# Layer 0's attention stream: every block of probabilities turned by a transpose, and the output projection over two groups of heads instead of four

## The chip, the core and the metric

The kernel runs on one NeuronCore of a Trainium2 chip. The core's engines work side by side and wait for each other by semaphores: TensorE (PE, matmuls into PSUM; PEld is its weight load), VectorE (DVE), ScalarE (ACT), GpSimd (POOL) and SyncE (SP, which issues DMAs). The metric is the device time of one execution in microseconds, the median of several runs. TensorE's clock is granted at one of two levels, 2.4 GHz (shown as 1.00) or 1.2 GHz (shown as 0.50).

## What is computed

A decoder of two layers on 4 sequences of 256 tokens, width 256, all in float32. Layer 0, which the change touches, begins with causal self-attention of 16 heads of width 16 and cross-attention of 8 heads of width 32:

```python
# self-attention, dk = 16, after rotary embedding of Q and K
scores = jnp.einsum('bhqd,bhkd->bhqk', Q, K) / dk ** 0.5
scores = jnp.where(causal, scores, -jnp.inf)
probs = jax.nn.softmax(scores, axis=-1)
attn = jnp.einsum('bhqk,bhkd->bhqd', probs, V)
attn = attn.swapaxes(1, 2).reshape(B, S, D)
return jnp.einsum('bsi,io->bso', attn, Wo)
...
x = _layernorm(x + _L0_attn_ref(x, ...), axis=-1)
x = _layernorm(x + _L0_xattn_ref(x, ctx_2048, ctx_2048, L0_xattn_gamma), axis=-1)
x = _layernorm(x + _L0_ffn_ref(x, ...), axis=-1)
```

Then come layer 1's attention (32 heads), an expert layer chosen by token, and a routed mixture of experts. They are not changed.

## The kernel before

Layer 0's attention has two parts. `project_0` makes Q, K and V of all 8 token tiles; `layer_0` is the stream that the change is about. After it follows `feed_forward_0`.

**Layout.** A head of width 16 is padded to 32 rows, so that four heads fill the 128 partitions: a *group* is four heads, a batch of the self-attention has four groups, a batch of the cross-attention (heads of 32) has two. `V[:, 4*b+g, kt, :]` holds for each key tile the values of a group, 32 columns a head, of which 16 are zeros: `project_0` clears V with one memset on POOL (L290) before ACT writes the 16 columns of each head (L319). `WO0` has the rows of the output weights padded in the same way, four groups of 128 rows.

**The stream.** `Layer0Plan` lists 16 groups of self-attention (4 batches) and then 8 of cross-attention. Each group is two *slots*, of two heads each, 48 slots in all (slots 0 to 31 self, 32 to 47 cross). Every engine runs through the slots in an order written out by hand, with a lag of two slots between scores and turns. For slot `t`:

- PE `score(t)` (L410): four products with 32 rows of the array each (one head, one query tile), in pairs into `psS`. A float32 product is two passes, each with its own weight load.
- DVE `peak(t)` (L487 self, L493 cross): adds the mask and takes the maximum, four operations with a read of `nm` each.
- ACT `exps(t)` (L584): four exponentials with their sums, then `keep(t-2)`.
- DVE `invert(t)` (L501): reciprocal of the sums; POOL `norm(t)` (L613) multiplies.
- PE `turn(t)` (L423, L425): turns the probabilities so that keys lie on partitions. A self slot has three 128x128 blocks for each of its two heads, a cross slot four. The blocks of the first head (`u == 0`) are transposes, those of the second are products with the identity.
- ACT `keep` (L593) copies the first head's blocks to `PT`, DVE `keep` (L509) the second's.
- PE `mix(t)` (L445): probabilities times V, four heads side by side in 32 columns of the array each, 256 query columns for key tile 0 and 128 for key tile 1 in the self-attention, 256 for both in the cross-attention.
- DVE `store` (L516 self, L520 cross): after both slots of a group it copies `psO` to `AT`, or adds the residual.

PE's order in a step is `score(t+1)`, `turn(t-2)`, then `output` if due, then `mix(t-4)`. `output` (L457) comes once for each batch, just before the first mix of the next: `AT` of four groups times `WO0`, 2 token tiles x 4 groups, waiting for the last group's store. DVE's `take` (L533) adds the residual and `measure` takes the statistics of the layer norm; POOL `root` (L620, L622) takes the root between two `norm`s. `psO` has two halves; `plan.unit[i]` numbers what goes into them, one unit a group and one an output, and is also the count that waits on the semaphore `mixed` use.

Of the kernel before, what the change touches and what calls it, by code (L numbers as in the profile page):

```python
# [165 lines left out]
def project_0(nc, c, XT, W0, QT, KT, V, WU, WD, identb, ternary, loads, load_w0, load_rest):  # L166
# [5 lines left out]
    with ExitStack() as stack:  # L172
# [114 lines left out]
        @block.gpsimd  # L287
        def _(pool):
            pool.memset(padded[:], 0.0)
            pool.memset(V[:], 0.0).then_inc(cleared, 1)  # L290
            pool.wait_ge(cleared, 1)
            for t in range(NT):
                pool.wait_ge(rot, 3 * (t + 1))
                need(pool, turned, t - 1)
                for a in range(2):
                    which = slice(a * 2 * P, (a + 1) * 2 * P)
                    pool.tensor_tensor(
                        padded[:, t % 2, a, :, 0:DK0].rearrange("p h (e j) -> p e h j", e=2),
                        T1[:, t % 2, which].rearrange("p (e h j) -> p e h j", e=2, h=H0),
                        T2[:, t % 2, which].rearrange("p (e h j) -> p e h j", e=2, h=H0),  # L300
                        ALU.add).then_inc(roped, 1)

        @block.scalar
        def _(act):
            load_w0(act)

            def keep(t):
                act.wait_ge(turned, t + 1)
                for a in range(2):
                    out = (QT, KT)[a].rearrange("p (b g) s -> p b g s", g=4)[:, t // 2, :,  # L310
                                                                             (t % 2) * P:(t % 2 + 1) * P]
                    last = nc.scalar.activation(out, psT[:, t % 2, a, :].rearrange("p (g s) -> p g s", g=4), ACT.Copy)
                last.then_inc(kept, 1)

            act.wait_ge(cleared, 1)
            for t in range(NT):
                act.wait_ge(v_made, t + 1)
                out = V.rearrange("p (b g) k (h d) -> p b g k h d", g=4, h=4)[:, t // 2, :, t % 2, :, 0:DK0]
                nc.scalar.activation(out, psV[:, t % 2, 0:D].rearrange("p (g h d) -> p g h d", g=4, h=4),  # L319
                                     ACT.Copy).then_inc(v_kept, 1)  # L320
                if t > 0:
                    keep(t - 1)
            keep(NT - 1)


class Layer0Plan:
# [6 lines left out]
    def __init__(self):  # L333
        order = (("self", 0), ("self", 1), ("self", 2), ("self", 3), ("cross", 0), ("cross", 1), ("cross", 2),
                 ("cross", 3))
        self.groups = [(kind, b, g) for kind, b in order for g in range(4 if kind == "self" else 2)]
        self.slots = 2 * len(self.groups)
        self.output_at = {}
        self.unit = []
        units = 0  # L340
        for i, (kind, b, g) in enumerate(self.groups):
            before = self.groups[i - 1] if i > 0 else None
            if before is not None and before[0] == "self" and before[2] == 3:
                self.output_at[i] = (before[1], units)
                units += 1
            self.unit.append(units)
            units += 1

# [10 lines left out]
def layer_0(nc, c, X, QT, KT, V, AT, WO0, CTX, CT, GM, loads):  # L359
# [7 lines left out]
    with ExitStack() as stack:  # L367
# [25 lines left out]
        def _(pe):  # L393
# [20 lines left out]
            def turn(t):  # L414
# [3 lines left out]
                for u in range(2):  # L418
                    need(pe, s["copied_a" if u == 0 else "copied_v"], t)
                    for qt, kt, at in blocks:  # L420
                        p = Pr[:, t % 4, 2 * u + qt, kt * P:(kt + 1) * P]
                        if u == 0:
                            last = nc.tensor.transpose(psT[:, u, at:at + P], p, c["ident"])  # L423
                        else:
                            last = nc.tensor.matmul(psT[:, u, at:at + P], p, c["ident"], start=True, stop=True)  # L425
                    last.then_inc(s["turned"], 1)

            def mix(t):
# [8 lines left out]
                for n in range(4):  # L437
                    rows = slice(n * 32, (n + 1) * 32)
                    if kind == "self":
                        v, at = V[:, 4 * b + g, kt, rows], kt * P  # L440
                        p = PT[:, i % 2, n, 0:S] if kt == 0 else PT[:, i % 2, n, S:S + P]
                    else:
                        v, at = CT[:, b, kt, g * P + n * 32:g * P + (n + 1) * 32], 0
                        p = PT[:, i % 2, n, kt * S:(kt + 1) * S]
                    last = nc.tensor.matmul(psO[rows, plan.unit[i] % 2, at:S], v, p,  # L445
                                            start=(kt == 0), stop=(kt == 1), skip_group_check=True)
                if kt == 1:
                    last.then_inc(s["mixed"], 1)

            def output(i):  # L450
                b, unit = plan.output_at[i]
                if b == 0:
                    pe.wait_ge(loads["wo0"], 16)
                pe.wait_ge(s["stored"], unit)
                for t in range(2):
                    for g in range(4):
                        last = nc.tensor.matmul(psO[:, unit % 2, t * D:(t + 1) * D],  # L457
                                                AT[:, 4 * b + g, t * P:(t + 1) * P], WO0[:, g, :],
                                                start=(g == 0), stop=(g == 3))
                last.then_inc(s["mixed"], 1)  # L460
# [17 lines left out]
        def _(dve):  # L478
# [24 lines left out]
            def keep(t):  # L503
                dve.wait_ge(s["turned"], 2 * t + 2)
                i = t // 2
                if i >= 2:
                    dve.wait_ge(s["mixed"], plan.unit[i - 2] + 1)
                w = plan.width(t)
                nc.vector.tensor_copy(PT[:, i % 2, 2 * (t % 2) + 1, 0:w], psT[:, 1, 0:w]).then_inc(s["copied_v"], 1)  # L509

            def store(i):
                kind, b, g = plan.groups[i]
                unit = plan.unit[i]
                dve.wait_ge(s["mixed"], unit + 1)
                if kind == "self":
                    nc.vector.tensor_copy(AT[:, 4 * b + g, :], psO[:, unit % 2, 0:S]).then_inc(s["stored"], 1)  # L516
                else:
# [10 lines left out]
            def take(i):  # L528
                b, unit = plan.output_at[i]
                if b == 0:  # L530
                    dve.wait_ge(loads["x"], 16)
                dve.wait_ge(s["mixed"], unit + 1)
                nc.vector.tensor_tensor(R[:, 2 * b:2 * b + 2, :], psO[:, unit % 2, :].rearrange("p (t d) -> p t d", t=2),  # L533
# [20 lines left out]
            for t in range(steps):  # L554
# [10 lines left out]
                m = t - LT - 4  # L565
                if 0 <= m < slots and m % 2 == 0:
                    store(m // 2)
# [9 lines left out]
        def _(act):  # L577
# [9 lines left out]
            def keep(t):  # L587
                act.wait_ge(s["turned"], 2 * t + 1)
                i = t // 2
                if i >= 2:  # L590
                    act.wait_ge(s["mixed"], plan.unit[i - 2] + 1)
                w = plan.width(t)
# [1626 lines left out]
def decoder(nc, x, xT, ctx, ctxT, tok, w0, wo0, gamma, wu, wd, had, w1, bqk, bv, wo1, bo1, sinks, gate,  # L2219
            w_in, w_out, c_in, c_out, table, out):  # L2220
    stack = ExitStack()
    with stack:
# [36 lines left out]
        with ExitStack() as layer0:  # L2259
            l0 = Store(nc, layer0)  # L2260
            CTX = l0.sb("CTX", [P, NT, D])
            WO0 = l0.sb("WO0", [P, 4, D])
            WU = l0.sb("WU", [P, KD, I0])
# [3 lines left out]
            with ExitStack() as attn0:  # L2267
                a0 = Store(nc, attn0)
                QT = a0.sb("QT", [P, 4 * B, S])
                KT = a0.sb("KT", [P, 4 * B, S])  # L2270
                V = a0.sb("V", [P, 4 * B, 2, P])
                AT = a0.sb("AT", [P, 4 * B, S])
                with ExitStack() as proj0:
# [111 lines left out]
def arrays_of(inputs):  # L2385
# [3 lines left out]
    wq, wk, wv = g["L0_attn_Wq"], g["L0_attn_Wk"], g["L0_attn_Wv"]  # L2389
    wo0 = np.zeros((4, 4, 32, D), np.float32)  # L2390
    wo0[:, :, 0:DK0] = g["L0_attn_Wo"].reshape(4, 4, DK0, D)
    flat = lambda a: a.reshape(D, -1)
# [6 lines left out]
        ctxT=ctx.transpose(0, 2, 1), tok=g["itok_BxS_13_99985"].reshape(NT, P).T,  # L2399
        w0=np.concatenate([split(wq), split(wk), wv], axis=1), wo0=wo0.reshape(4, P, D),  # L2400
        gamma=g["L0_xattn_gamma"].reshape(1, 1), wu=g["L0_ffn_w_up"].T, wd=g["L0_ffn_w_down"].T, had=had,
# [26 lines left out]
```

## Time and profile before

| | us |
|---|---|
| median of 3 runs | 877.35 (875.77 to 881.85) |
| the profiled execution | 880.92, its span 879.1 |
| layer 0's stream, first score to last statistics | 42.5 to 213 |
| PE busy over the span | 765.6 (87%) |
| DVE / ACT / POOL busy | 613.6 / 456.1 / 431.9 |

Busy time of PE counts from the issue of a matmul to its modelled end; matmuls overlap, so 100% does not mean that the array is at its peak. The distance between the starts of two matmuls tells more. Brackets at the end of a timeline row give the idle time of that engine just before and what ended it. The granted clock (PEclk) is a mean over the stretch.

### The profile page before, as it was taken

To read this page: it belongs to the slowest core of one execution; us is meant where nothing else is said; L and a number is where in the kernel's file an instruction comes from. 1 tells how busy PE (TensorE), PEld (TensorE's weight loads), DVE (VectorE), ACT (ScalarE), POOL (GpSimd) and SP (SyncE) were. 2 spreads that over 40 slices of the span, in tenths; PEclk is the share of its full clock that TensorE was granted. 3 is DMA by queue.
4 is the path that set the end of the run, shared out by engine and by line. 5 is a ranking of instruction groups with operands and counts; after the bars stand their busy time and mean duration, and the time that the engine had idled before them with its cause. 6 is when DMAs were issued, how large, how long until landed. Compare 5 with 4: busy or idle time off the path is not lost. (4 is left out here: it accounts for less than half of the span.)

```text
span 879.1 us, 18142 instructions
## 1 busy us (share of the span) xinstructions
PE 765.6 (87%) x5770; PEld 481.4 (55%) x5770; DVE 613.6 (70%) x2060; ACT 456.1 (52%) x1447; POOL 431.9 (49%) x427
## 2 busy tenths in 40 slices
PE   6899899987877999999999999999574489999944
PEld 4566666665753444555555555688454445555523
DVE  2656776695694778788888888442355768889856
ACT  2366776573422000688888888300232077777734
POOL 4344654563001666566666666100540368888840
PEclk9869999998986999999999999999795589999976
DMA  9400000000000667500000000160268322222225
GB/s 324 186 1 1 2 2 1 1 2 1 0 1 27 166 161 181 150 1 1 1 1 1 1 2 1 37 270 19 79 242 215 119 62 75 77 75 75 75 73 175
DMA packets 32493, 63.44 MB, mean 72 GB/s; under 512 B 6592, under 2 KB 21324, under 8 KB 31536
## 3 DMA queue, kind: packets, MB, share of 16 engines
q1 hardware_dynamic: 20960, 41.67, 14.8%
q0 software_dynamic: 4896, 11.95, 4.3%
q10 hardware_dynamic: 6544, 8.67, 3.7%
q8 instruction: 48, 0.79, 0.4%
q14 instruction: 45, 0.37, 0.1%
HBM read 41.27 MB, written 9.84 MB: 58 GB/s over the span
## 5 line engine op out<-in xcount | busy, mean ns | idle before, releaser
L1398 ACT ACTIVATE a_room<-a_room,a_nm 128x257 f32<-128x257 f32 x256 | 127.3, 499 | 100.6 <-DVE a_nm L1241 99.8
L1440 POOL TENSOR_TENSOR a_room<-a_room,a_rd 128x1024 f32<-128x1024 f32 x64 | 121.3, 1895 | 65.8 <-DVE a_rd L1249 65.4
L1241 DVE CUSTOM_DVE_ANT_0 a_room<-a_ps,table,NSK 128x256 f32<-128x256 f32 x256 | 107.8, 478 | 0.7 <-PE a_ps L1100 0.4
L584 ACT ACTIVATE l_Pr<-l_Sm,l_nm 128x128 f32<-128x128 f32 (+1 forms) x192 | 88.3, 461 | 36.1 <-DVE l_nm L487 22.0
L613 POOL TENSOR_TENSOR l_Pr<-l_Pr,l_rd 128x256 f32<-128x256 f32 (+1 forms) x80 | 82.0, 1043 | 50.4 <-DVE l_rd L501 50.3
L1100 PEld LDWEIGHTS a_ps<-room 64*128 64x128 f32 x512 | 44.1, 186 | 53.2 <-issue 48.5
L1180 PE MATMUL a_ps<-a_room,W 128*128 128x512 f32 x160 | 72.5, 612 | 0.8 <-ACT a_room L1412 0.8
L1100 PE MATMUL a_ps<-room 64*128 64x256 f32 x512 | 72.3, 402 | 0.5 <-DVE a_nm L1241 0.5
L1221 DVE SCALAR_TENSOR_TENSOR a_room<-a_ps,BQK,table 128x512 f32<-128x512 f32 x80 | 56.4, 746 | 22.9 <-PE a_ps L1180 22.9
L1115 PE MATMUL a_ps<-table,a_room 128*128 128x128 f32 x512 | 69.7, 279 | 1.1 <-ACT a_room L1407 1.1
L1446 POOL TENSOR_TENSOR a_room<-a_room 128x512 f32<-128x512 f32 x20 | 25.4, 1271 | 90.3 <-DVE a_room L1221 90.3
L1128 PE MATMUL a_psO<-a_room,room 128*64 128x512 f32 x256 | 68.8, 617 | 0.0
L1115 PEld LDWEIGHTS a_ps<-table,a_room 128*128 128x128 f32 x512 | 55.0, 141 | 22.4 <-issue 21.9
L2087 ACT ACTIVATE ex_w_in<-room 128x384 f32 x120 | 53.7, 514 | 25.9 <-issue 25.9
L1256 DVE COPY a_room<-a_ps 128x512 f32<-128x512 f32 x64 | 44.2, 691 | 20.0 <-PE a_ps L1115 14.0
L509 DVE COPY l_PT<-l_psT 128x384 f32<-128x384 f32 (+1 forms) x48 | 28.7, 597 | 41.9 <-PE l_psT L425 41.7
L1143 PE MATMUL a_ps<-W,room 128*128 128x256 f32 x256 | 56.8, 381 | 0.0
L1143 PEld LDWEIGHTS a_ps<-W,room 128*128 128x128 f32 x256 | 48.2, 190 | 9.5 <-issue 3.2
L1180 PEld LDWEIGHTS a_ps<-a_room,W 128*128 128x128 f32 x160 | 31.3, 197 | 39.6 <-issue 39.6
L1965 POOL DMA_INDIRECT pairs<-ex_y,ti_index x40 | 42.4, 1060 | 21.3 <-issue 10.7
L2135 DVE COPY ex_c_in<-room 128x512 f32 x120 | 47.6, 450 | 5.7 <-issue 5.7
L1398 ACT ACTIVATION_READ_ACCUMULATOR a_room<-a_room,a_nm 128x1 f32 x256 | 47.8, 187 | 0.0
(312 smaller groups left out, 1778.8 us busy)
## 6 DMA issues: line engine op xcount, KB each, us to landing
room<-a_room SPq DMA_DIRECT2D x96, 64.0 KB, 2.1
room<-a_room ACTq DMA_DIRECT2D x96, 64.0 KB, 2.1
room<-in_w_in SPq DMA_DIRECT2D x1, 6144.0 KB, 17.5
room<-in_c_in SPq DMA_DIRECT2D x1, 4096.0 KB, 13.4
room<-pairs SPq DMA_DIRECT2D x8, 512.0 KB, 8.8
W<-in_w SPq DMA_DIRECT2D x1, 3072.0 KB, 12.8
room<-in_w_out SPq DMA_DIRECT2D x1, 3072.0 KB, 20.4
W<-in_wo SPq DMA_DIRECT2D x1, 2048.0 KB, 8.4
```

Of the source, the lines that this page charges most:

```text
L584: nc.scalar.activation(Pr[:, t % 4, n, 0:n_keys], Sm[:, t % 2, n, 0:n_keys], ACT.Exp, bias=nm[:, t % 2, n:n + 1], scale=-1.0, accum_out=de ...
L613: last = pool.tensor_tensor(p, p, r.unsqueeze(2).to_broadcast([P, n, n_keys]), ALU.mult)
L1100: last = nc.tensor.matmul(psS(t)[:, u, qt, :], QT[rows, kv, t % 2, b, qt * P:(qt + 1) * P], KT[rows, kv, b, :], start=True, stop=True, ski ...
L1115: last = nc.tensor.transpose(psT[:, u, kt, qt * P:(qt + 1) * P], Pr[:, t % 4, 2 * u + qt, kt * P:(kt + 1) * P], c["ident"])
L1128: last = nc.tensor.matmul(ends_ps[h * D1:(h + 1) * D1, g % 2, :], V[:, g, kt, :], halves[:, h, kt, :], start=(kt == 0), stop=(kt == 1))
L1143: last = nc.tensor.matmul(psY(t), QT[:, i // 2, i % 2, t // 2, (t % 2) * P:(t % 2 + 1) * P], WO1[:, i, :], start=(i == 0), stop=(i == 2 * ...
L1180: last = nc.tensor.matmul(ps[:, i % 3, e, :], W1[:, k, (2 * g + e) * P:(2 * g + e + 1) * P], XT[:, k, n * 512:(n + 1) * 512], start=(k == ...
L1221: last = nc.vector.scalar_tensor_tensor(out=T[:, i % 2, part, :].rearrange("p (b s) -> p b s", b=2), in0=ps[:, i % 3, e, :].rearrange("p ( ...
L1241: nc.vector.tensor_tensor_reduce(out=Sm[:, t % 2, n, 0:S], in0=psS(t)[:, n // 2, n % 2, :], in1=c["window"][:, n % 2, :], scale=-1.0, scal ...
L1398: nc.scalar.activation(Pr[:, t % 4, n, :], Sm[:, t % 2, n, :], ACT.Exp, bias=nm[:, t % 2, n:n + 1], scale=-1.0, accum_out=den[:, t % 2, n: ...
L1440: pool.tensor_tensor(p, p, rd[:, t % 2, :].unsqueeze(2).to_broadcast([P, 4, S]), ALU.mult).then_inc(normed, 1)
L2087: nc.scalar.activation(w_in[:, k % 2, n], W.w_in[:, bass.ds(held[k][n] * KD, KD), :], ACT.Copy).then_inc(s["w_in"], 1)
```

## The change

- `turn`: both heads' blocks are turned by transposes; the products with the identity (L425) are gone.
- `V` grows from 32 to 48 columns a head, zeros, 16 values, zeros. `mix` takes 32 of them, either values then zeros (even groups) or zeros then values (odd groups). Two groups add up in the same 32 rows of `psO` (`start` only at the first group of a pair, `stop` at the second), so that 128 partitions hold eight heads without padding.
- So `AT` has two pieces a batch, not four, a store comes after each second group only, `WO0` has two groups of 128 rows without padding, and `output` multiplies 2 token tiles x 2 pieces.
- POOL clears the two sides of V by two strided memsets, not all of it by one.
- `plan.unit` now counts halves of `psO` in use (one for a pair of groups), and a new `plan.event` counts increments of `mixed`.

```diff
             pool.memset(padded[:], 0.0)
-            pool.memset(V[:], 0.0).then_inc(cleared, 1)
+            sides = V.rearrange("p c k (h d) -> p (c k h) d", h=4)
+            pool.memset(sides[:, :, 0:DK0], 0.0)
+            pool.memset(sides[:, :, 2 * DK0:3 * DK0], 0.0).then_inc(cleared, 1)
             pool.wait_ge(cleared, 1)
...
                 act.wait_ge(v_made, t + 1)
-                out = V.rearrange("p (b g) k (h d) -> p b g k h d", g=4, h=4)[:, t // 2, :, t % 2, :, 0:DK0]
+                out = V.rearrange("p (b g) k (h d) -> p b g k h d", g=4, h=4)[:, t // 2, :, t % 2, :, DK0:2 * DK0]
                 nc.scalar.activation(out, psV[:, t % 2, 0:D].rearrange("p (g h d) -> p g h d", g=4, h=4),
...
         self.output_at = {}
-        self.unit = []
-        units = 0
+        self.unit, self.event = [], []
+        units, events = 0, 0
         for i, (kind, b, g) in enumerate(self.groups):
...
             if before is not None and before[0] == "self" and before[2] == 3:
-                self.output_at[i] = (before[1], units)
+                self.output_at[i] = (before[1], units, events)
                 units += 1
+                events += 1
             self.unit.append(units)
-            units += 1
+            self.event.append(events)
+            units += self.closes(i)
+            events += 1
+
+    def closes(self, i):
+        kind, b, g = self.groups[i]
+        return kind == "cross" or g % 2 == 1
+
+    def opens(self, i):
+        kind, b, g = self.groups[i]
+        return kind == "cross" or g % 2 == 0
...
                         p = Pr[:, t % 4, 2 * u + qt, kt * P:(kt + 1) * P]
-                        if u == 0:
-                            last = nc.tensor.transpose(psT[:, u, at:at + P], p, c["ident"])
-                        else:
-                            last = nc.tensor.matmul(psT[:, u, at:at + P], p, c["ident"], start=True, stop=True)
+                        last = nc.tensor.transpose(psT[:, u, at:at + P], p, c["ident"])
                     last.then_inc(s["turned"], 1)
...
                     if kind == "self":
-                        v, at = V[:, 4 * b + g, kt, rows], kt * P
+                        from_column = n * 3 * DK0 + (DK0 if g % 2 == 0 else 0)
+                        v, at = V[:, 4 * b + g, kt, from_column:from_column + 2 * DK0], kt * P
                         p = PT[:, i % 2, n, 0:S] if kt == 0 else PT[:, i % 2, n, S:S + P]
...
                     last = nc.tensor.matmul(psO[rows, plan.unit[i] % 2, at:S], v, p,
-                                            start=(kt == 0), stop=(kt == 1), skip_group_check=True)
+                                            start=(kt == 0 and plan.opens(i)), stop=(kt == 1 and plan.closes(i)),
+                                            skip_group_check=True)
                 if kt == 1:
...
             def output(i):
-                b, unit = plan.output_at[i]
+                b, unit, event = plan.output_at[i]
                 if b == 0:
...
                 for t in range(2):
-                    for g in range(4):
+                    for j in range(2):
                         last = nc.tensor.matmul(psO[:, unit % 2, t * D:(t + 1) * D],
-                                                AT[:, 4 * b + g, t * P:(t + 1) * P], WO0[:, g, :],
-                                                start=(g == 0), stop=(g == 3))
+                                                AT[:, 2 * b + j, t * P:(t + 1) * P], WO0[:, j, :],
+                                                start=(j == 0), stop=(j == 1))
                 last.then_inc(s["mixed"], 1)
...
                 if i >= 2:
-                    dve.wait_ge(s["mixed"], plan.unit[i - 2] + 1)
+                    dve.wait_ge(s["mixed"], plan.event[i - 2] + 1)
                 w = plan.width(t)
...
                 unit = plan.unit[i]
-                dve.wait_ge(s["mixed"], unit + 1)
+                dve.wait_ge(s["mixed"], plan.event[i] + 1)
                 if kind == "self":
-                    nc.vector.tensor_copy(AT[:, 4 * b + g, :], psO[:, unit % 2, 0:S]).then_inc(s["stored"], 1)
+                    nc.vector.tensor_copy(AT[:, 2 * b + g // 2, :], psO[:, unit % 2, 0:S]).then_inc(s["stored"], 1)
                 else:
...
             def take(i):
-                b, unit = plan.output_at[i]
+                b, unit, event = plan.output_at[i]
                 if b == 0:
                     dve.wait_ge(loads["x"], 16)
-                dve.wait_ge(s["mixed"], unit + 1)
+                dve.wait_ge(s["mixed"], event + 1)
                 nc.vector.tensor_tensor(R[:, 2 * b:2 * b + 2, :], psO[:, unit % 2, :].rearrange("p (t d) -> p t d", t=2),
...
                 m = t - LT - 4
-                if 0 <= m < slots and m % 2 == 0:
+                if 0 <= m < slots and m % 2 == 0 and plan.closes(m // 2):
                     store(m // 2)
...
                 if i >= 2:
-                    act.wait_ge(s["mixed"], plan.unit[i - 2] + 1)
+                    act.wait_ge(s["mixed"], plan.event[i - 2] + 1)
                 w = plan.width(t)
...
             CTX = l0.sb("CTX", [P, NT, D])
-            WO0 = l0.sb("WO0", [P, 4, D])
+            WO0 = l0.sb("WO0", [P, 2, D])
             WU = l0.sb("WU", [P, KD, I0])
...
                 KT = a0.sb("KT", [P, 4 * B, S])
-                V = a0.sb("V", [P, 4 * B, 2, P])
-                AT = a0.sb("AT", [P, 4 * B, S])
+                V = a0.sb("V", [P, 4 * B, 2, 4 * 3 * DK0])
+                AT = a0.sb("AT", [P, 2 * B, S])
                 with ExitStack() as proj0:
...
     wq, wk, wv = g["L0_attn_Wq"], g["L0_attn_Wk"], g["L0_attn_Wv"]
-    wo0 = np.zeros((4, 4, 32, D), np.float32)
-    wo0[:, :, 0:DK0] = g["L0_attn_Wo"].reshape(4, 4, DK0, D)
+    wo0 = g["L0_attn_Wo"].reshape(2, 2, 4, DK0, D).transpose(0, 2, 1, 3, 4)
     flat = lambda a: a.reshape(D, -1)
...
         ctxT=ctx.transpose(0, 2, 1), tok=g["itok_BxS_13_99985"].reshape(NT, P).T,
-        w0=np.concatenate([split(wq), split(wk), wv], axis=1), wo0=wo0.reshape(4, P, D),
+        w0=np.concatenate([split(wq), split(wk), wv], axis=1), wo0=wo0.reshape(2, P, D),
         gamma=g["L0_xattn_gamma"].reshape(1, 1), wu=g["L0_ffn_w_up"].T, wd=g["L0_ffn_w_down"].T, had=had,
...
```

## Rows read from the trace of the kernel before

**Rows 1.** Stretches: length, busy us (count) of PE, PEld, DVE, ACT, POOL; PEclk, DMA.

```profile
42.50:49.40 6.90, 4.95 (x33) 2.89 (x33) 3.11 (x21) 3.85 (x17) 2.00 (x3) 0.50 0.02 4
49.40:58.80 9.40, 9.40 (x45) 7.48 (x43) 4.13 (x26) 6.58 (x27) 4.45 (x6) 0.50 0.01 3
59.70:209.20 149.50, 135.51 (x1229) 95.42 (x1229) 109.55 (x499) 102.19 (x389) 81.69 (x86) 1.00 0.01 1
226.90:230.30 3.40, 1.15 (x12) 0.87 (x10) 0.79 (x2) 2.56 (x3) 0.00 (x0) 1.00 0.00 0
230.40:233.60 3.20, 3.20 (x14) 2.66 (x12) 2.67 (x9) 2.02 (x3) 0.00 (x0) 0.50 0.00 0
```

**Rows 2.** PE's timeline, low clock: start, us, engine, line, operation, output<-input.

```profile
53.05 0.90 PE L423 MATMUL l_psT<-table,l_Pr 128*128 128x128 f32 x3
53.74 1.49 PE L425 MATMUL l_psT<-table,l_Pr 128*128 128x128 f32 x6
55.16 1.65 PE L410 MATMUL l_psS<-KT,QT 32*128 32x128 f32 x8
56.74 0.90 PE L423 MATMUL l_psT<-table,l_Pr 128*128 128x128 f32 x3
...
58.85 1.00 PE L445 MATMUL l_psO<-l_PT,V 128*32 128x256 f32 x8
59.79 0.38 PE L410 MATMUL l_psS<-KT,QT 32*128 32x128 f32 x2
```

**Rows 3.** Instructions on psT and psO: count, then ns min/median/max, first and last start.

```profile
L425 PE MATMUL l_psT<-table,l_Pr x320: 275/275/421, 50.1 to 207.6; 128*128 128x128 f32 x160
L423 PE MATMUL l_psT<-table,l_Pr x160: 272/273/474, 49.4 to 206.7; 128*128 128x128 f32 x160
...
L457 PE MATMUL l_psO<-WO,AT x64: 379/379/483, 80.1 to 163.9; 128*128 128x256 f32 x64
```

**Rows 4.** PE's timeline, high clock, one self slot.

```profile
98.97 0.52 PE L423 MATMUL l_psT<-table,l_Pr 128*128 128x128 f32 x3
99.33 0.83 PE L425 MATMUL l_psT<-table,l_Pr 128*128 128x128 f32 x6
100.09 0.64 PE L445 MATMUL l_psO<-l_PT,V 128*32 128x256 f32 x8
...
101.52 0.55 PE L423 MATMUL l_psT<-table,l_Pr 128*128 128x128 f32 x3
```

**Rows 5.** Timelines of ACT and DVE, high clock, self slots.

```profile
101.47 0.40 ACT L584 ACTIVATE l_Pr<-l_Sm,l_nm 128x128 f32<-128x128 f32 x1 [0.22 <-DVE l_nm L487]
...
103.91 0.40 ACT L584 ACTIVATE l_Pr<-l_Sm,l_nm 128x128 f32<-128x128 f32 x1 [0.19 <-DVE l_nm L487]
...
105.60 0.41 DVE L516 COPY AT<-l_psO 128x256 f32<-128x256 f32 x1
```

**Rows 6.** PE's timeline around two outputs and after the second.

```profile
77.79 0.55 PE L423 MATMUL l_psT<-table,l_Pr 128*128 128x128 f32 x3
...
106.07 3.72 PE L457 MATMUL l_psO<-WO,AT 128*128 128x256 f32 x16 [0.98 <-DVE AT L516]
109.72 0.64 PE L445 MATMUL l_psO<-l_PT,V 128*32 128x256 f32 x8
...
117.39 0.52 PE L423 MATMUL l_psT<-table,l_Pr 128*128 128x128 f32 x3 [0.62 <-POOL l_Pr L613]
```

**Rows 7.** PE's timeline, turns of the cross-attention (slots 38, 42, 47).

```profile
176.34 0.66 PE L423 MATMUL l_psT<-table,l_Pr 128*128 128x128 f32 x4
...
190.34 0.66 PE L423 MATMUL l_psT<-table,l_Pr 128*128 128x128 f32 x4 [0.51 <-POOL l_Pr L613]
...
206.29 0.66 PE L423 MATMUL l_psT<-table,l_Pr 128*128 128x128 f32 x4
```

**Rows 8.** POOL's timeline at the start.

```profile
2.49 3.51 POOL L290 MEMSET V<- 128x4096 f32 x1
12.87 0.72 POOL L297 TENSOR_TENSOR p_padded<-p_T 128x256 f32<-128x256 f32 x1 [6.86 <-DVE p_T L272]
```

## Prediction

> **What bounds the kernel now.** I read the granted clock by stretches first, because TensorE (PE) is what the change edits and its operations take twice as long at one level as at the other [rows 1]. The reader is to see this: while layer 0's stream starts (42.5 to 58.8 us) the clock is 0.50, the lower level (1.2 GHz); from 59.7 to 209.2 it is 1.00 (2.4 GHz) throughout. Then the matmuls in order of time, once at each level [rows 2, 4], give the length of a slot (two heads). Then what paces ACT and DVE [rows 5], the output projection [rows 6] and the cross attention [rows 7].
>
> In the low stretch PE is the bound: it is busy 9.40 of 9.40 us [rows 1], a slot is 56.74 - 53.05 = 3.69 us [rows 2]. In the high stretch two loops tie. PE's is 101.52 - 98.97 = 2.55 us in a slot whose mix has 256 columns [rows 4]; every second slot mixes 128, half of the 0.43 us that two passes of 256 take when four run side by side, so 2.34 there and 2.45 in the mean. The other loop is ACT's four exponentials, the reciprocal, the next peak and the next exponential, 103.91 - 101.47 = 2.44 us, at whose end ACT waits 0.19 us for DVE's `nm` [rows 5]. Once a batch everything stops: PE waits 0.98 us for `AT`, then does 3.65 us of output projection (106.07 to 109.72) [rows 6]. In the cross attention the nine slots from 176.34 to 206.29 average 3.33 us, and before a turn there PE waits 0.51 us for POOL [rows 7].
>
> **Part 1, products to transposes.** A product is two passes with two weight loads, a transpose one: 320 against 160 for the same 160 blocks [rows 3]. High clock: nine passes, six of them products, run from 98.97 to 100.09 [rows 4]; six products took 0.76 of that with the hand-over to the mix, at 0.112 each 0.67 us. A transpose takes (99.33 - 98.97)/3, at most 0.12, so three take 0.33: 0.34 us less in a self slot, 0.46 in a cross slot (eight passes become four). The self gain is almost wholly covered: the ACT-DVE loop of 2.44 us stays, so a slot falls by some hundredths of a us (DVE's store of 0.41 us in every second round also goes, see part 2), and over the 20 or so undisturbed slots I take 1 us, between 0 and the 6.8 of an uncovered 20 x 0.34. In the cross part POOL and DVE pace many slots; of 16 x 0.46 = 7.4 us (0 the other bound) I take 2, because the row nearest, a turn started by POOL, shows PE not to be the last [rows 7]. Tail: 0.5 us.
>
> **Part 2, output over two groups.** 64 passes become 32 [rows 3]: 3.65/2 = 1.8 us less per batch at the high clock. This is on the path, since nothing else runs meanwhile. The turns just before and after it are also on it, 2 x 0.34. So 2.5 us x 4 batches = 10 us. The wait for `AT` stays: the store still follows DVE's copy of the second half of that turn. Eight of 16 stores (0.41 us) go [rows 5]. The `event` numbers keep each wait at the same work as before; two groups now share a half of `psO`, which asks for no earlier store than now. Mix matmuls keep shape and number: their 32 columns include 16 zeros.
>
> **Part 3, clearing.** The one memset of 3.51 us becomes two over as many elements, strided; it ends at 6.0 and POOL then idles 6.86 us until 12.87 [rows 8], so even at twice the time it is hidden; without that cover it would cost at most 3.5 us. WO0's DMA halves on SP's queue, and all behind it only moves forward.
>
> **The clock.** Parts 1 to 3 at the clocks of now: three starting slots save 3 x 0.64 = 1.9 us (six products at 0.213 are 1.28, three transposes 0.64 [rows 2]); sum 1.9 + 1 + 10 + 2 + 0.5 = 15.4 us. But the clock is not given. Look at what PE did before it rose [rows 1, 2]: from 42.5 scores alone (32 rows of the array), low; from 49.4 to 58.8 scores, transposes and products without a pause, still low; at 58.85 the first mix joined, and within 0.85 us it rose. Products, 6 x 0.213 of each 3.69 us, are the only full-array arithmetic in there, and they go. What stays is narrower arithmetic than before, at a stretch that already did not suffice; the turns to come are all transposes. And it can fall inside a stream: before the low stretch 230.4 to 233.6 PE had been busy 1.15 of 3.4 us, with four transposes and the first of a set of narrow-type products [rows 1]. In the stream of now, the pauses after each output (0.62 us before the turn at 117.39 [rows 6]) are survived with products beside them; that cover is taken away.
>
> The Trainium skill says in "TensorE: Matmul & The Clock Gate", section "Part 4: PE-mode transpose", that the full clock does not engage for transposes, which don't count as PE work in the same way; the trace agrees so far as that PE full of work, part of it transposes, stayed at 0.50 for 9.4 us. By that rule the time is that of the forecast or of rival 3 below; by passes alone, that of rival 1.
>
> Price of the low clock, from [rows 2]: a self turn of six transposes 0.27 + 5 x 0.213 = 1.33 us, the hand-over 0.14, scores 56.745 - 55.16 = 1.58, a mix 59.79 - 58.85 = 0.93 with 256 columns and half of it with 128, mean 0.72: 3.77 us a slot, 1.32 over 2.45. PE is then the only bound, as ACT's loop is 2.44. A cross slot: 8 transposes 1.76, 0.14, scores 4 x 0.427 and the 0.3 us that the self scores take beyond their 2 x 0.213 + 2 x 0.427, together 2.0, mix 0.93: 4.83, 1.5 over 3.33. The clock stays low from the start until something dense comes; the first such thing is the output, 8 x 0.427 = 3.4 us of full-array work, which I expect to bring it back, as the step up at 59.7 came with arithmetic added to an already busy PE.
>
> **Low throughout (rival 3)**: turns 0 to 2 at 3.69 - 0.64 = 3.05 us bring turn 2 to 55.5; 29 self slots x 3.77 = 109; 16 cross slots x 4.83 = 77; four outputs at 3.4 + 1.2 wait + 0.5 = 20.4; so turn 47 starts at 262.5 against 206.3 [rows 7], the tail is 1.3 longer: +57.5, 935 us.
>
> **Forecast**: low until output 0; each of the four outputs brings it back, it holds for about four turns, until the pause of the restart, then falls and stays low to the next output, after the fourth to the end. Each high spell gives back 4 x 1.32 = 5.3 us (the last 4 x 1.5 = 6.0), less 0.9 each because the pause of the restart shows again: 18.3 in all. 935 - 18 = 917 us. The sum is made on the profiled execution (880.9 us, span 879.1); applied to the median 877.35, which lies 3.6 below it, and rounded.
>
> **Rivals.**
> 1. The clock moves as now: 877.35 - 15.4 = 862. For: mixes are there to help it up from 58 on. Against: the stretch 49.4 to 58.8. It decides if the clock is 1.00 by 60 us and never falls before 205. The skill's "Perfetto Trace Analysis", section "Transposes", which asks for transposes in place of matmuls since they skip arithmetic, points here.
> 2. It returns with output 0 and holds: turn 10 comes at 55.5 + 8 x 3.77 = 85.6, not 77.8 [rows 6], so +7.8; then three events 7.5, slots 1, cross 2, tail and turn 0.8, together 11.3: 874. For: 2.4 GHz held through all pauses so far.
> 4. As 2, but it falls in the cross attention, where PE waits for POOL: +0 to 16 x 1.5 = +24 on 874, middle 885 to 890.
>
> **Chances**: forecast 0.46, rival 3 0.13, rival 4 0.11, rival 2 0.13, rival 1 0.17. The range 866 to 938 holds forecast, 2, 4, half of 3 and the edge of 1. Forecast alone: 900 to 930. A measurement of this kernel tells about 1% from no change: faster (below 868.6) 0.17; slower (above 886.1) 0.70, that is forecast, 3 and 4; same 0.13.
>
> **What would show it.** Right: granted clock 0.50 past 60 us up to the first output near 84; slots of 3.7 to 3.8 us with PE always busy; each output followed by a few slots of 2.4; cross slots near 4.8. Part 1 wrong if transposes at 1.00 take more than 0.12 each; part 2 if an output at 1.00 is not near 1.8 us. The forecast is wrong as a whole if the scores, mixes and transposes of 58 to 84 raise the clock without an output, or if the pauses after an output leave it at 1.00.

## The result, and the profile after

| | before | after |
|---|---|---|
| median of 20 runs, us | 877.32 (875.28 to 883.27) | 882.12 (865.07 to 896.34) |
| ratio, from the runs within 1.5% of the fastest | | 0.993 [0.990, 0.995] |
| the profiled execution, its span | 880.92, 879.1 | 880.97, 879.2 |
| PE / DVE / ACT / POOL busy | 765.6 / 613.6 / 456.1 / 431.9 | 758.4 / 611.0 / 457.2 / 432.1 |

The interval leaves out each run that is more than 1.5% above its kernel's fastest, here 14 of the 20 of after, so it describes after's short runs alone. The medians stand at 1.0055, the interval at 0.993: the two disagree in sign and both are within 1%, so no change is shown either way. 917 us was forecast, and slower.

The spread is a finding in itself: before keeps within 8 us, after goes over 31. Each run lists its span and mean granted clock, so the time at the lower level is 2 x (1 - clock) x span: 133 us in the run of 865.07 (clock 0.923), about 225 in that of 896.34 (0.874). Over the 20 runs the time is 818 + 0.352 us for each us at the lower level, with a correlation of 0.995. The price is the prediction's: 1.32 us lost in a slot of 3.77, 0.350. The execution profiled before the change had 141 us at the lower level (clock 0.920). Put into the line of after, that gives 868 us, which is an estimate: with the clock of before the change would have been worth about 13 us of the 880.92.

The granted clock by stretches, to be laid beside [rows 1] (length, busy us (count) of PE, PEld, DVE, ACT, POOL; PEclk, DMA):

```profile
45.30:86.70 41.40, 40.05 (x218) 24.41 (x218) 20.23 (x116) 26.85 (x105) 18.66 (x23) 0.50 0.01 1
86.80:89.50 2.70, 2.70 (x7) 2.17 (x8) 1.02 (x8) 1.86 (x8) 1.61 (x2) 0.50 0.00 0
89.70:171.40 81.70, 67.82 (x629) 42.41 (x629) 61.11 (x294) 59.59 (x231) 45.44 (x53) 1.00 0.01 2
171.60:178.30 6.70, 6.70 (x38) 3.60 (x38) 5.01 (x14) 3.78 (x14) 3.60 (x2) 0.50 0.00 0
178.50:202.10 23.60, 17.92 (x160) 10.87 (x156) 21.85 (x86) 17.23 (x63) 14.42 (x11) 1.00 0.00 1
202.30:209.00 6.70, 6.07 (x36) 3.77 (x40) 3.24 (x9) 1.34 (x3) 3.31 (x4) 0.50 0.01 2
```

The reader is to see three things. The start lasts at 0.50 until the first output (it begins at 86.8, the clock rises at 89.6), 30 us longer than before. Then 1.00 holds for 81.7 us, through three restarts, that is, the short pauses of PE 8 to 11 us after an output begins. At the fourth, the one after output 3, it falls, comes back by itself 6.7 us later, and falls once more for 6.7 us late in the cross attention.

The fall at the fourth restart, and the same place before, where the clock stayed at 1.00 (turn 37 in both):

```profile
168.79 1.13 PE L423 MATMUL l_psS<-CTX,X 32*128 32x256 f32 x8 [0.57 <-DVE l_nm L505]
170.85 1.36 PE L435 MATMUL l_psT<-table,l_Pr 128*128 128x128 f32 x8 [0.93 <-POOL l_Pr L625]
...
173.23 0.66 PE L423 MATMUL l_psT<-table,l_Pr 128*128 128x128 f32 x4 [0.93 <-POOL l_Pr L613]
```

The first two rows are of after, the last one of before: the same wait for POOL, 0.93 us. This place repeats in every profile of this case. In all eleven profiled executions in which a cross turn is eight transposes, the clock falls within 1.0 us of the start of turn 37, for about 3.4 or 6.8 us. In the three in which it has twelve full-array passes (before, out_only, transposes_twice) it stays at 1.00. The four more passes also fill most of the pause ahead of the scores: in before PE's mix of 170.41 lasts to 171.05 and the scores start at 171.17.

The timeline of PE of the same kernel: a slot at the lower level and one at the higher ([rows 2, 4] of before), then outputs 0 and 1 ([rows 6]):

```profile
57.42 1.54 PE L435 MATMUL l_psT<-table,l_Pr 128*128 128x128 f32 x6
...
61.06 1.54 PE L435 MATMUL l_psT<-table,l_Pr 128*128 128x128 f32 x6
...
84.19 1.54 PE L435 MATMUL l_psT<-table,l_Pr 128*128 128x128 f32 x6
86.80 3.35 PE L469 MATMUL l_psO<-WO,AT 128*128 128x256 f32 x8 [1.07 <-DVE AT L528]
...
102.59 0.84 PE L435 MATMUL l_psT<-table,l_Pr 128*128 128x128 f32 x6 [0.48 <-ACT l_PT L605]
...
105.02 0.85 PE L435 MATMUL l_psT<-table,l_Pr 128*128 128x128 f32 x6 [0.37 <-ACT l_PT L605]
...
111.71 1.99 PE L469 MATMUL l_psO<-WO,AT 128*128 128x256 f32 x8 [0.98 <-DVE AT L528]
113.63 0.64 PE L456 MATMUL l_psO<-l_PT,V 128*32 128x256 f32 x8
...
119.42 0.92 PE L423 MATMUL l_psS<-KT,QT 32*128 32x128 f32 x8 [0.91 <-DVE l_nm L499]
120.96 0.85 PE L435 MATMUL l_psT<-table,l_Pr 128*128 128x128 f32 x6 [0.62 <-ACT l_PT L605]
```

A slot at 0.50 with the narrow mix is 61.06 - 57.42 = 3.64 us, with PE not idle in it. At 1.00 it is 105.02 - 102.59 = 2.43 us, and PE now waits 0.37 to 0.48 us in each for the other loop: the saving per slot is wait, as said. The output is 113.63 - 111.71 = 1.92 us against 3.65, and the restart behind it has its two pauses of 0.91 and 0.62 us, at 1.00.

Turn 10 starts at 84.19 against 77.79 [rows 6], 6.4 us late. After that the kernel gains: turn 19 is 3.9 us late, turn 27 1.5, turn 35 1.9 early. The cross attention and the tail spend this again: turn 47 starts at 205.84 against 206.29 [rows 7], 0.5 early, and both spans end within 0.1 us of each other.

### The profile page after: what moved, and what is told of

It is laid out like the page before. It is cut to its first block and busy times, and to the rows that moved or that the text cites. A ratio compares the mean times of both kernels' runs of the same rounds, so it can differ in the third digit from the quotient of the medians.

```text
span 879.2 us, 17751 instructions
## 1 busy us (share of the span) xinstructions
PE 758.4 (86%) x5578; PEld 463.9 (53%) x5578; DVE 611.0 (69%) x2052; ACT 457.2 (52%) x1447; POOL 432.1 (49%) x428
## 5 line engine op out<-in xcount | busy, mean ns | idle before, releaser
L1452 POOL TENSOR_TENSOR a_room<-a_room,a_rd 128x1024 f32<-128x1024 f32 x64 | 121.3, 1895 | 66.6 <-DVE a_rd L1261 66.4
L435 PE MATMUL l_psT<-table,l_Pr 128*128 128x128 f32 x320 | 55.5, 323 | 13.3 <-POOL l_Pr L625 8.2
L435 PEld LDWEIGHTS l_psT<-table,l_Pr 128*128 128x128 f32 x320 | 41.9, 164 | 35.1 <-issue 18.0
```

What stands on the lines that cost most here:

```text
L1452: pool.tensor_tensor(p, p, rd[:, t % 2, :].unsqueeze(2).to_broadcast([P, 4, S]), ALU.mult).then_inc(normed, 1)
```

## The experiments

There are twelve experiments in three sets, each set on a chip of its own beside the kernel before, and a comparison holds within a set: out_only, turn_only, after_again and start_products beside 892.83 us; transposes_twice, restart_held, warm_start and after_third beside 880.03; start_scores and after_look1 to after_look3 beside 878.33. Even the kernel before is not without the longer course: one of its seven runs in the third set took 892.45 us at a mean clock of 0.888. `t` is the slot, `u` the head of the slot.

**The two halves of the change.** out_only is the kernel after, with the second head turned by products again:

```diff
-    last = nc.tensor.transpose(psT[:, u, at:at + P], p, c["ident"])
+    if u == 1:
+        last = nc.tensor.matmul(psT[:, u, at:at + P], p, c["ident"], start=True, stop=True)
+    else:
+        last = nc.tensor.transpose(psT[:, u, at:at + P], p, c["ident"])
```

> The changed kernel with the second head's blocks turned by products with the identity again, as before the change: only the output over two groups and its stores are new. Theory A (the products kept the clock at 2.4 GHz; taking them away costs, the shorter output gains): the clock moves as in the kernel before, the output is 1.8 us shorter four times and the stores save some tenths, so 877.3 - 8 = 869 us, with as little spread between runs as the kernel before. Theory B (the spread and the lost gain of the changed kernel come from the output or the stores, not from the turns): as long and as spread as the changed kernel, 865 to 896.

Measured 884.31 (882.89 to 891.9), ratio 0.991 [0.988, 0.994], 8.5 us faster. turn_only is the kernel before with the line of the transpose alone, its output over four groups:

```diff
-    if u == 0:
-        last = nc.tensor.transpose(psT[:, u, at:at + P], p, c["ident"])
-    else:
-        last = nc.tensor.matmul(psT[:, u, at:at + P], p, c["ident"], start=True, stop=True)
+    last = nc.tensor.transpose(psT[:, u, at:at + P], p, c["ident"])
```

> The kernel before with all blocks turned by transposes, output over four groups. Theory A: the clock stays low until the first output, near 85 us, which costs 6 to 7 us; the turns beside the four outputs give back 2.7, the cross attention 0 to 2; without a later fall 879 us, with falls up to 895, and the runs spread by 1 to 3 per cent. Theory B: no effect of the turns on the clock: rise near 60 us, 877.3 - 5 = 872.

Measured 911.42 (903.29 to 917.37), ratio 1.019 [1.015, 1.023], 18.6 us slower. Its stretches (PE alone: length, busy, PEclk, DMA):

```profile
45.60:89.80 44.20, 42.79 (x225) 0.50 0.01 1
90.00:100.00 10.00, 8.48 (x76) 1.00 0.00 0
100.20:123.90 23.70, 22.72 (x120) 0.50 0.01 2
124.10:134.10 10.00, 8.48 (x82) 1.00 0.00 0
134.30:158.00 23.70, 22.72 (x112) 0.50 0.01 1
```

Its first three outputs are at 87.1, 120.3 and 153.7. Twice this is the forecast's course: low until an output, 10 us high, low from the pause of the restart to the next output. After the third output the clock holds until 195.6. It is the turns that lose, and they lose by the clock: its six runs have 0.879 to 0.899 where before has 0.919 to 0.930. The whole change again, as after_again:

> The changed kernel once more, for a second profile. Theory A: another course of the granted clock in the stream than in the first profile, and the time of each run follows from how long the clock was low: each us at 1.2 GHz in the stream costs about a third of a us. Theory B: the same course of the clock, and the time differs elsewhere.

Measured 900.04 (882.57 to 909.41, the clock from 0.915 down to 0.879 in the same order), 7.2 us above before on that chip. The profiled execution is a short one: low 39.5 to 66.6, then four stretches of 3.4, 6.8, 3.4 and 3.4 us.

**What the products did for the clock.** start_products is after with products in the first five slots only (`if u == 1 and t < 5` in the diff of out_only):

> The changed kernel with products with the identity for the second head in the first five turns only (turns 0 to 4), transposes after. Theory A: the clock rises near 60 us as before the change, which gives back the 6 to 7 us of the start: 877.3 - 10 = 867 us if it holds, and most runs are below those of the changed kernel. Theory B: no gain over the changed kernel, since the products only add passes: median near 882.

Measured 881.48 (879.66 to 884.52), ratio 0.988 [0.985, 0.991], 11.4 us faster, and its six runs keep within 5 us. The clock is at 1.00 from 58.7:

```profile
41.60:58.50 16.90, 15.03 (x79) 0.50 0.01 2
58.70:160.90 102.20, 85.94 (x804) 1.00 0.01 2
161.10:164.30 3.20, 3.20 (x19) 0.50 0.00 0
```

So most of the loss lies at the start: 18.6 us of the median go with fifteen products. The fall at turn 37 stays (161.0). But is it the products, or only what they add to PE's work? transposes_twice is after with each block of the second head transposed twice, as many full-array passes as out_only, none of them a product:

```diff
-    last = nc.tensor.transpose(psT[:, u, at:at + P], p, c["ident"])
+    for _ in range(1 + u):
+        last = nc.tensor.transpose(psT[:, u, at:at + P], p, c["ident"])
```

> The changed kernel in which each block of the second head is turned twice, by two transposes into the same place, so that PE has as many passes as with products. Theory A (what keeps the clock is the arithmetic of the products, transposes do less for it): still 1.2 GHz from the start to the first output, near 80 to 88 us, and the time as long and as spread as the changed kernel's, ratio to before 0.99 to 1.02. Theory C (any pass would do, PE only has to be full): rise near 60 us, ratio 0.99 with little spread.

Measured 874.63 (868.95 to 876.25), ratio 0.993 [0.990, 0.995]. The stretches of transposes_twice:

```profile
41.00:64.60 23.60, 20.25 (x112) 0.50 0.01 2
64.80:208.00 143.20, 125.51 (x1172) 1.00 0.01 2
```

and those of out_only:

```profile
41.10:64.80 23.70, 20.37 (x113) 0.50 0.00 1
65.00:208.10 143.10, 126.19 (x1170) 1.00 0.01 2
```

The two agree to 0.2 us, and their turns 0 to 35 to 0.3 us. One profile of the start alone would not tell, since after itself rose at 65.0 in after_third, on the same chip. The runs do: the eleven of transposes_twice have a mean clock of 0.917 to 0.929, the six of out_only 0.918 to 0.929, and after's go down to 0.874. And neither falls at turn 37, which after does each time. The premise of the prediction falls here: in this stream a second transpose did for the clock what a product's passes did. It is no gain in time over after's short runs (after_third has 864.91 and 870.47).

Would any further work do? start_scores is after with the second head's scores computed twice in slots 1 to 8, four more passes a slot of 32 rows each:

```diff
-    last = nc.tensor.matmul(psS[:, 2 * (t % 2) + u, qt, 0:n_keys], q, k, ...)
+    for _ in range(2 if u == 1 and 1 <= t < 9 else 1):
+        last = nc.tensor.matmul(psS[:, 2 * (t % 2) + u, qt, 0:n_keys], q, k, ...)
```

> The changed kernel in which the scores of the second head of a slot are computed twice in slots 1 to 8: four more passes a slot, over 32 rows of the array, where the experiment with doubled transposes added three over all 128 rows. Theory E (what brings the clock back in the stream are passes over the whole array, transposes as well as products; narrow ones do little): rise no earlier than in the changed kernel, 65 to 90 us, and PE's slots at 1.2 GHz longer by 0.6 us, so ratio to before 1.00 to 1.03. Rival C (any pass would do): rise near 60 us as with doubled transposes, ratio 0.99.

Measured 893.83 (884.99 to 901.97), ratio 1.021 [1.011, 1.031].

```profile
41.20:88.80 47.60, 46.17 (x239) 0.50 0.00 1
89.00:126.30 37.30, 30.58 (x288) 1.00 0.01 2
126.50:140.00 13.50, 13.50 (x80) 0.50 0.00 1
```

Its output 0:

```profile
93.66 1.97 PE L470 MATMUL l_psO<-WO,AT 128*128 128x256 f32 x8 [1.07 <-DVE AT L529]
```

PE was busy 46.17 of 47.6 us, and the clock stayed at 0.50 until 88.9. That is about where four of after's six profiled executions have it (89.6 to 93.3), and all four runs have a clock of 0.900 or less. The added scores did not do what the added transposes did. The ratio rests on two of the four runs. The profile shows one thing more: 88.9 lies 4.8 us ahead of output 0 (93.66), behind the last doubled scores, and the later stretch ends at 140.0, ahead of output 2 (144.91). The clock comes back without an output too.

**The pause of the restart.** restart_held is turn_only with products in slots 12, 13, 20, 21, 28 and 29:

```diff
+    if u == 1 and 8 <= t < 32 and t % 8 in (4, 5):
+        last = nc.tensor.matmul(psT[:, u, at:at + P], p, c["ident"], start=True, stop=True)
+    else:
         last = nc.tensor.transpose(psT[:, u, at:at + P], p, c["ident"])
```

> The kernel with transposes alone and the output over four groups (turn_only), with products with the identity again in the two turns around each pause after an output (turns 12, 13, 20, 21, 28, 29). Theory A (the pause of PE after an output is where the clock falls, and products beside it held it): low until the first output as in turn_only, then no fall before the cross attention; two low stretches of 24 us less at about 0.35 us each, so 17 us less than turn_only, ratio to before 1.00. Rival D (it is the mean of the whole stream that lets the clock fall, not the pause): falls as in turn_only, ratio 1.02.

Measured 880.82 (875.3 to 887.5), ratio 1.003 [1.000, 1.007].

```profile
58.10:102.30 44.20, 38.31 (x370) 1.00 0.01 2
102.50:105.70 3.20, 3.13 (x7) 0.50 0.02 5
105.90:129.60 23.70, 19.94 (x192) 1.00 0.00 1
129.80:133.00 3.20, 3.20 (x8) 0.50 0.01 3
```

The two low stretches of 24 us are gone; 3.4 us at the waits before outputs 1 and 2 remain, and later 3.4 us at turn 37 and twice more. This kernel's start was short too (1.00 from 58.1) though it has no products there, so not all of the gain over turn_only belongs to the restarts. Nor are the products' passes the only difference there: with them PE's pause before the scores of the restart is 0.57 us, in turn_only 0.91, and which of the two held the clock was not separated.

**A better version.** warm_start is start_products with six products into an unused place, two after the scores of each of the first three steps:

```diff
                 if t + 1 < slots:
                     score(t + 1)
+                if t < 3:
+                    for _ in range(2):
+                        nc.tensor.matmul(psO[:, 1, 0:S], c["ident"], c["causal"], start=True, stop=True)
```

> start_products with six more products of the identity with 256 columns (two in each of the first three steps, into a half of psO that nothing reads before it is overwritten), where PE waits for the first probabilities. Theory A: the clock rises by 50 to 56 us instead of 59 to 65, three to eight us less at 1.2 GHz, 1 to 3 us less than start_products, ratio to before 0.985. Against: the extra work delays the first scores and turns, ratio 0.99.

Measured 866.06 (861.89 to 870.82), ratio 0.987 [0.983, 0.990], 14.0 us faster than before.

```profile
39.50:46.10 6.60, 5.17 (x28) 0.50 0.00 1
46.30:158.70 112.40, 95.55 (x880) 1.00 0.01 2
```

The clock is back at 46.3, before the first turn (49.99), not at 50 to 56 as expected. Against start_products no gain is shown: the intervals, 0.987 and 0.988, overlap.

**The kernel after, four times more.** Its executions differ, so more of them were profiled.

> The changed kernel once more, for a third profile. Theory A: where a run is near its upper end (2 per cent above before), the clock fell after an output and stayed low to the next, as in turn_only; where it is near its lower end, the clock was low only at the start and for two short stretches in the cross attention. The length of the low stretches gives the time at 0.35 us per us.

Measured 864.91, 870.47, 880.44 and one run of 3907.33 that nothing explains. The profiled one (870.47) was short: low 41.1 to 65.0, later 3.4, 6.8, 3.4, 6.8 and 3.4 us.

> The changed kernel, one look, to see the course of the clock in a run near the upper end of its times. If this run is over 1 per cent above before: low from the start to the first output and again after one or more outputs (theory A for turn_only, holds for this kernel too). If it is below before: low to 60 to 90 us and only short stretches later.

> As the look before: a long run has low stretches of 20 us or more after outputs; a short run has none.

> As the two looks before: a long run has low stretches of 20 us or more after outputs; a short run has none.

883.28, 887.0 and 886.6 us at clocks of 0.894, 0.891 and 0.892, all three with a long low start. None is 1% above before on that chip (878.33), so the condition of the first expectation was not met; low stretches after an output came all the same, one after output 0 in each, 13.6 to 23.9 us long. after_look2 by stretches, then its PE after output 0:

```profile
41.10:92.10 51.00, 48.05 (x262) 0.50 0.00 1
92.30:98.90 6.60, 5.07 (x52) 1.00 0.00 0
99.10:122.80 23.70, 22.72 (x121) 0.50 0.01 1
123.00:180.80 57.80, 48.18 (x443) 1.00 0.01 2
181.00:187.70 6.70, 6.70 (x38) 0.50 0.00 0
```

```profile
86.98 3.75 PE L469 MATMUL l_psO<-WO,AT 128*128 128x256 f32 x8 [1.07 <-DVE AT L528]
...
97.13 0.92 PE L423 MATMUL l_psS<-KT,QT 32*128 32x128 f32 x8 [0.91 <-DVE l_nm L499]
98.67 1.19 PE L435 MATMUL l_psT<-table,l_Pr 128*128 128x128 f32 x6 [0.62 <-POOL l_Pr L625]
```

With output 0 1.00 comes back, PE pauses 0.91 and 0.62 us at the restart, and at 99 the clock falls until output 1: the forecast's course to the letter, but once. The restarts after outputs 1 and 2 lose nothing; the one after output 3 loses 6.7 us (181.0). after_look3 has the same stretches within 0.3 us; after_look1 fell from 100.0 to 113.7 and came back 4.8 us ahead of output 1 (118.44), with nothing in between but scores, transposes and mixes.

## Why the prediction was wrong

**Part 2, right.** Output 1.92 us for 1.8; 2.4 to 3.4 us a batch for 2.5; turn 10 to turn 35 gained 8.3 us where three such events and the slots give 8.5; out_only gave 8.5 us for 8 expected. AT's wait stayed (0.98 us), and only eight stores are left. **Part 3, right**: two clearings of 1.80 us, and POOL idles 6.58 us behind them ([rows 8] had 6.86):

```profile
2.49 1.80 POOL L291 MEMSET V<- 128x2048 f32 x1
4.24 1.80 POOL L292 MEMSET V<- 128x2048 f32 x1
12.62 1.40 POOL L299 TENSOR_TENSOR p_padded<-p_T 128x256 f32<-128x256 f32 x2 [6.58 <-DVE p_T L272]
```

**Part 1, right in size.** Slots at 1.00 went from 2.45 to 2.43 us, the rest is PE's wait for ACT; slots at 0.50 are 3.64 and 4.07 us, mean 3.86 for 3.77. Parts 1 to 3 together were put at 15.4 us; the estimate from the runs above is 13.

**The clock.** Right: that the clock would be lost at the start when the products go; that it would stay 0.50 past 60 to output 0, in four of after's six profiled executions; that 1.00 comes back with an output (there, and three times in turn_only, 2.8 to 5.3 us after it begins); that the pause of the restart can make it fall. turn_only has this round twice, after_look2 and after_look3 once.

Wrong, first, was the premise from which the forecast was carried on: that products are what holds the clock, and transposes do little. Transposes in their place gave the same stretches (transposes_twice and out_only). The Trainium skill's rule in "TensorE: Matmul & The Clock Gate", section "Part 4: PE-mode transpose", that transposes do not engage the full clock, is not borne out for these float32 transposes: doubled transposes in place of the products left the mean clock at 0.917 to 0.929, the products at 0.918 to 0.929. What the change took away from a slot was three of nine full-array passes, whatever their kind.

Wrong, second and decisive in the sum, was the step "holds for about four turns ... then falls and stays low to the next output, after the fourth to the end". It took what was plausible at one restart for a rule at all four, and took the output for the only way back. In the profiled execution the clock fell at the fourth restart alone, and came back by itself after 6.7 us where the forecast had it low to the end; in after_look1 to after_look3 it fell at the first and the fourth. After_look1 and start_scores came back between outputs. In the cross attention (12 slots at 1.5 us in the sum once the high spell after the fourth output is given back, 18 us) the six profiled executions have stretches of 3.4 or 6.8 us, one to three of them. In numbers: the forecast lies 55 us above rival 1's 862, all of it clock, and the profiled execution has 35 us more at the lower level than before (176 against 141), at 0.352 each 12 us. Why the stretches after turn 37 end by themselves was not tried. The price of a low cross slot was right: 4.91 us from scores to scores (173.16 to 178.07) for 4.83.

The profiled execution is rival 4's course: a return with output 0, then falls in the cross attention where PE waits for POOL, at a smaller price than the middle that it was given. Measured, it is 6.4 us late by turn 10 (7.8 said for output 0), gains 8.3 by turn 35 (8.5 said), loses 1.5 from there to turn 47 and 0.5 behind it, +0.1 in all. The last two were put at gains of 2 and 0.8; two stretches of 6.7 us at 0.35, 4.7 us, fill the difference, so the account closes to 0.1 us, if those two gains are taken as forecast; they were not measured by themselves. Rival 1's gain of 15.4 us for a clock as before was near: 13 by the estimate above, and warm_start, whose clock is like that of before (0.920 to 0.933), has 14.0 with its extra passes.

The forecast also wanted one course. This kernel has several, and the time follows which one it takes. By the six profiled executions of after: low from the start until 65 to 67 us in two, to output 0 in four, and three of these four fall once more at the first restart. Why an execution takes one or the other was not found; the program and its data are the same, and the spread shows on one chip. Nor is it settled why the pauses hold in after where they failed twice in turn_only. The halves add up to -8.5 + 18.6 = +10.1, both together gave +7.2 on that chip, but after_again's own six runs spread over 27 us, so this difference says nothing; turn_only was profiled only once.

## What to carry to other kernels

Work on PE that looks useless can be what keeps its clock: before full-array passes are removed, read the granted clock by stretches. A long stretch at 1.00 does not make the removal safe: before stood at 1.00 from 59.7 to 213.2 us through every pause, and each kernel without the extra passes fell at the same pause of it (turn 37). Put such passes back just where the clock is low (here fifteen products in the first five slots turned 7.2 us lost into 11.4 won on the same chip, and brought the spread from 27 us to 5). When the mean clock of a kernel's runs differs, one profile shows one course; look at several before writing down a cause.

## What the runs showed of the hardware

- PE busy was no sign of a high clock: 48.05 of 51.0 us busy at 0.50 (after_look2), with scores, narrow mixes and transposes.
- Four more 32-row passes in each of eight slots left the clock at 0.50 until 88.9, with mean clocks of 0.879 to 0.900 in four runs; three more full-array passes a slot, product or transpose, had it at 1.00 from 64.8, with mean clocks of 0.917 to 0.929 in 17 runs. Without either it rose at 65 to 67 us in two executions and at 89.6 to 93.3 in four.
- Pauses of PE of 0.57 and 0.93 us before turn 37: the clock fell within 1.0 us of the turn's start in all eleven profiled executions with eight full-array passes in the turn. It stayed at 1.00 in the three with twelve, which had the 0.93 us but hardly a pause before it.
- The low level was left with an output (nine times in after, after_look1 to 3 and turn_only, 2.8 to 5.3 us after it began) and without one (start_scores at 88.9 and 140.1, after_look1 at 113.7).
- Two products more in each of the first three steps, and 1.00 came at 46.3 us instead of 58.7, in one profile each.
- The same program took 865 to 896 us on one chip, 0.352 us for each us at the lower level.
